# Third attention: tiles turned by ordinary matmuls with the identity as moving operand, and one step later

## What is computed

```python
Q, K, V = (proj(Wq), proj(Wk), proj(Wv))
scores = jnp.einsum('bhqd,bhkd->bhqk', Q, K) / SCALE
rel_k = pek[idx]
scores = scores + jnp.einsum('bhqd,qkd->bhqk', Q, rel_k) / SCALE
scores = jnp.where(causal[None, None], scores, -jnp.inf)
attn = jax.nn.softmax(scores, axis=-1)
out = jnp.einsum('bhqk,bhkd->bhqd', attn, V)
rel_v = pev[idx]
out = out + jnp.einsum('bhqk,qkd->bhqd', attn, rel_v)
```

## Time and profile before

| | us |
|---|---|
| median of 3 runs | 4647.89 |
| lowest and highest | 4644.03, 4655.52 |
| the profiled execution, its own time | 4653.93 |
| its span | 4652.1 |
| PE busy in the span | 3257.9 (70%) |
| DVE busy | 2404.9 (52%) |
| ACT busy | 1877.1 (40%) |

### The profile page before, as it was taken

How to read it: one execution, slowest core, us unless ns; L and a number is a source line. 1 busy time by engine, 2 the same in 40 slices (tenths; PEclk the granted TensorE clock), 3 DMA queues, 4 the chain that set the end, 5 groups by cost and what they waited for, 6 DMA issues and landing times. The chain is left out here.

```text
span 4652.1 us, 70787 instructions
## 1 busy us (share of the span) xinstructions
PE 3257.9 (70%) x22883; PEld 1799.3 (39%) x22883; DVE 2404.9 (52%) x4948; ACT 1877.1 (40%) x4450; POOL 684.5 (15%) x964
## 2 busy tenths in 40 slices
PE   5588544374435777778775777777783288849998
PEld 3344233253322444444443333333332122227776
DVE  4565466455655666666642445445455488821111
ACT  2355322211113455554542444444441177723332
POOL 2100000120003444444422000000000300000000
PEclk8798766686667899999986666666665599969999
DMA  4323000000001000000004777777772522220000
GB/s 118 64 48 62 23 0 0 8 1 5 0 9 47 17 17 9 17 17 17 17 9 138 188 190 192 190 192 191 193 195 72 137 42 53 40 69 1 0 0 18
DMA packets 423549, 303.19 MB, mean 65 GB/s; under 512 B 60175, under 2 KB 396234, under 8 KB 423250
## 3 DMA queue, kind: packets, MB, share of 16 engines
q1 hardware_dynamic: 414034, 278.32, 24.3%
q0 software_dynamic: 6912, 18.88, 1.3%
q10 hardware_dynamic: 2304, 2.36, 0.2%
HBM read 148.98 MB, written 133.18 MB: 61 GB/s over the span
## 5 line engine op out<-in xcount | busy, mean ns | idle before, releaser
L1139 DVE TENSOR_REDUCE a_soft_NM<-a_soft_s_ps 128x2 f32<-128x1024 f32 (+3 forms) x512 | 514.5, 1021 | 204.2 <-PE a_soft_s_ps L1074 132.3
L1173 ACT ACTIVATE a_soft_PTS<-a_soft_st_ps 128x512 f32<-128x512 f32 (+3 forms) x1024 | 458.3, 522 | 148.1 <-PE a_soft_st_ps L1050 100.9
L464 PE MATMUL a_soft_pt_ps<-net_ident,a_soft_PR 128*128 128x128 f32 x1280 | 328.7, 369 | 110.0 <-ACT a_soft_PTS L566 103.5
L612 ACT ACTIVATE a_soft_PR<-a_soft_s_ps,a_soft_least 128x128 f32<-128x128 f32 (+3 forms) x512 | 263.7, 526 | 342.3 <-DVE a_soft_least L587 237.9
L1045 PE MATMUL a_soft_st_ps<-a_soft_QS,a_soft_KS 50*128 50x512 bf16 (+4 forms) x1024 | 258.7, 360 | 59.4 <-ACT a_soft_PTS L1173 33.3
L1954 ACT ACTIVATE f_run_HT<-f_run_h_ps 128x512 f32<-128x512 f32 x256 | 152.8, 597 | 290.7 <-PE f_run_h_ps L1921 290.7
L1968 DVE SCALAR_TENSOR_TENSOR net_X<-f_run_y_ps,f_COEF,net_X 128x128 f32 x256 | 72.1, 344 | 381.2 <-PE f_run_y_ps L1930 381.2
L464 PEld LDWEIGHTS a_soft_pt_ps<-net_ident,a_soft_PR 128*128 128x128 f32 x1280 | 182.6, 180 | 208.7 <-ACT a_soft_PR L612 146.2
L1930 PEld LDWEIGHTS f_run_y_ps<-f_W,f_run_HT 128*128 128x128 f32 x2048 | 237.5, 192 | 26.8 <-issue 26.8
L1087 PE MATMUL a_soft_o_ps<-a_soft_PTS,a_soft_VR 128*32 128x512 f32 (+3 forms) x2048 | 242.6, 548 | 0.1
L2104 PE MATMUL f_run_ps<-f_run_WQKV,f_run_HT 128*128 128x512 f32 x384 | 229.6, 689 | 15.5 <-DVE f_run_RS L1402 8.3
(11 more groups left out here) (356 smaller groups left out, 6517.4 us busy)
## 6 DMA issues: line engine op xcount, KB each, us to landing
a_soft_BIAS<-skew_d SPq DMA_DIRECT2D x256, 191.0 KB, 4.2
band_d<-a_soft_PR SPq DMA_DIRECT2D x256, 191.0 KB, 3.7
skew_d<-a_soft_RS SPq DMA_DIRECT2D x128, 256.0 KB, 4.4
a_soft_PB<-band_d SPq DMA_DIRECT2D x128, 256.0 KB, 3.1
a_soft_QS<-query_rows_d SPq DMA_DIRECT2D x32, 384.0 KB, 9.6
query_rows_d<-a_proj_PARTS SPq DMA_DIRECT2D x72, 128.0 KB, 3.5
query_rows_d<-a_proj_PARTS POOLq DMA_DIRECT2D x72, 128.0 KB, 3.0
key_rows_d<-a_proj_PARTS SPq DMA_DIRECT2D x72, 128.0 KB, 3.9
```

Source lines behind the costliest of these rows:

```text
L464: last = pe.transpose(pt_ps[:, slot, kb * P:(kb + 1) * P], PR[:, n % NPR, OFF + kb * P:OFF + (kb + 1) * P], ident[:])
L612: act.activation(PR[:, n % NPR, OFF:OFF + width(j)], s_ps[:, n % 4, 0:width(j)], ACT.Exp, bias=least[:, n:n + 1], scale=-1.0).then_inc(pro ...
L1139: dve.tensor_reduce(NM[:, T % 2, j, p, :], s_ps[:, ring["s", a] % 2, :, 0:width(j)], AX.X, ALU.max, negate=True).then_inc(max_ready, 1)
L1173: act.activation(PTS[:, T % 2, 2 * p + par, kb, q0:S], st_ps[:, e % 3, q0:S], ACT.Exp, scale=scale).then_inc(probs_ready, 1)
```

## The change

Two things are changed in `relative_heads`:

1. `turn` and `turn_band` call `pe.matmul(out, lhsT=tile, rhs=ident, start=True, stop=True)` in place of `pe.transpose(out, tile, ident)`. The result is the same turned tile.
2. The turn in step n is that of step n-3 (LAG = 3). With it the tiles per position change: step j = 0 turns two tiles (one of them was three), j = 1 three, j = 2 four beside the band's four, j = 3 one. The semaphore counts in `missing`, `before`, `through`, `pv` and in ACT's wait before it writes `PR` follow, and so do the last turns after the last quad.

```diff
+    LAG = 3
     def missing(seq, slots):
-        return sum(m < seq and m % 2 in slots for m in (0, 1, 2, 7))
+        return sum(m < seq and m % 2 in slots for m in (0, 1, 2, 3, 7))
     def before(hd, pos):
-        return 5 * hd + pos - 4
+        return 5 * hd + pos - 5
     def through(qd, h, pos):
-        return 10 * qd + (5 * h + pos) // 2 - 2
+        return 10 * qd + (5 * h + pos) // 2 - 2 - (5 * h + pos) % 2
@@ turn
-                    last = pe.transpose(pt_ps[:, slot, kb * P:(kb + 1) * P], PR[:, n % NPR, OFF + kb * P:OFF + (kb + 1) * P], ident[:])
+                    last = pe.matmul(pt_ps[:, slot, kb * P:(kb + 1) * P], PR[:, n % NPR, OFF + kb * P:OFF + (kb + 1) * P], ident[:],
+                                     start=True, stop=True)
@@ turn_band
-                    last = pe.transpose(pt_ps[:, slot, j * P:(j + 1) * P], PB[:, hb % 2, j, :], ident[:])
+                    last = pe.matmul(pt_ps[:, slot, j * P:(j + 1) * P], PB[:, hb % 2, j, :], ident[:], start=True, stop=True)
@@ pv
-            def pv(qd, sl, kb, turned=2):
+            def pv(qd, sl, kb, turned=(2, 1)):
-                    pe.wait_ge(pt_copied[0], 10 * (qd + 1) + turned)
-                    pe.wait_ge(pt_copied[1], 10 * (qd + 1) + turned)
+                    pe.wait_ge(pt_copied[0], 10 * (qd + 1) + turned[0])
+                    pe.wait_ge(pt_copied[1], 10 * (qd + 1) + turned[1])
@@ quad of PE
-                    if n >= 2:
-                        turn(qd, n - 2, h, pos, qd)
+                    if n >= LAG:
+                        turn(qd, n - LAG, h, pos, qd)
                     elif prev:
-                        turn(qd - 1, n + 14, h, pos, qd)
+                        turn(qd - 1, n + 16 - LAG, h, pos, qd)
@@ last of PE
-                turn(4 * B - 1, 14, 0, 0, 4 * B)
-                turn(4 * B - 1, 15, 0, 1, 4 * B)
+                turn(4 * B - 1, 13, 0, 0, 4 * B)
+                turn(4 * B - 1, 14, 0, 1, 4 * B)
                 turn_band(4 * B - 1, 2, 0, 4 * B)
-                turn_band(4 * B - 1, 3, 0, 4 * B, 3)
+                turn(4 * B - 1, 15, 0, 3, 4 * B)
+                turn_band(4 * B - 1, 3, 0, 4 * B, 4)
@@ copies (n - 2 and n + 14 become n - LAG and n + 16 - LAG), last of DVE
+                copy_out(dve, 0, 4 * B, 0, 4, 1, 3, None)
@@ quad of ACT
-                        act.wait_ge(pt_ready, before(4 * qd + h - 2, 4 + j))
+                        act.wait_ge(pt_ready, before(4 * qd + h - 2, (5, 6, 7, 9)[j]))
```

More of the change, by code:

```diff
@@ L527, in last @@
             def last():
-                turn(4 * B - 1, 14, 0, 0, 4 * B)
-                turn(4 * B - 1, 15, 0, 1, 4 * B)
+                turn(4 * B - 1, 13, 0, 0, 4 * B)
+                turn(4 * B - 1, 14, 0, 1, 4 * B)
                 turn_band(4 * B - 1, 2, 0, 4 * B)
-                turn_band(4 * B - 1, 3, 0, 4 * B, 3)
+                turn(4 * B - 1, 15, 0, 3, 4 * B)
+                turn_band(4 * B - 1, 3, 0, 4 * B, 4)
                 for kb in range(NPT):
-                    pv(4 * B - 1, 1, kb, 0)
+                    pv(4 * B - 1, 1, kb, (1, -1))
             for hd in range(3):
@@ L548, in copies @@
                         copy_out(eng, slot, qd, h, pos, sl if h >= 2 else 1 - sl, (h + 2) % 4, None)
-                elif n >= 2:
-                    copy_out(eng, slot, qd, h, pos, sl, (n - 2) // 4, n - 2)
+                elif n >= LAG:
+                    copy_out(eng, slot, qd, h, pos, sl, (n - LAG) // 4, n - LAG)
                 elif prev:
-                    copy_out(eng, slot, qd, h, pos, 1 - sl, 3, n + 14)
+                    copy_out(eng, slot, qd, h, pos, 1 - sl, 3, n + 16 - LAG)
         def copy_out(eng, slot, now, h, pos, sl, head, n):
@@ L591, in last @@
             def last():
-                copy_out(dve, 0, 4 * B, 0, 0, 1, 3, 14)
+                copy_out(dve, 0, 4 * B, 0, 0, 1, 3, 13)
                 copy_out(dve, 0, 4 * B, 0, 2, 1, 2, None)
+                copy_out(dve, 0, 4 * B, 0, 4, 1, 3, None)
             batches(quad, last, dve)
@@ L640, in last @@
             def last():
-                copy_out(act, 1, 4 * B, 0, 1, 1, 3, 15)
-                copy_out(act, 1, 4 * B, 0, 3, 1, 3, None)
+                copy_out(act, 1, 4 * B, 0, 1, 1, 3, 14)
+                copy_out(act, 1, 4 * B, 0, 3, 1, 3, 15)
                 store(4 * B - 1, 1, B, 0)
```

## The result

The changed kernel takes 4779.2 us (median of four runs, 4772.3 to 4787.8) against 4646.0 for the kernel before, measured beside it: 1.028 times, 95% interval 1.026 to 1.030, or 130 us more. The forecast was 4631, the range 4615 to 4700. Sign and size were both wrong.

A forecast was written before the change was run, and what follows sets the result against it. SP's queue, waiting for band-store landings, was taken as the bound. Of its 25.1 us waiting for exponentials about 20 go, against 3 us added: net -17 us, 4631 on the median, range 4615 to 4700.

The forecast's parts named there:

- That SP bounds the kernel before: Third attention: SP's queue, waiting 354.8 us of 951 for band-store landings, sets the round; at most 29 us can be won.
- 0.1 us a quad, 3 us in all: Cost in the sum for the early step and the longer step with the band, against about 20 us won.
- Two records a tile: Turned tiles: an ordinary f32 matmul makes two PE records, not one; +0.11 us a tile at upper clock, +0.2 at lower.
- their 6 to 11 us of PE a quad: PE's extra time for 56 turned tiles a quad: +6.2 us all at the upper level, +11 all at the lower.
- LAG 3: I take 0: Turning tiles one step later: worth 0 to 0.3 us a quad, taken as 0, since ACT's slot copies still hold PE.
- at step 2 ... 0.5 to 1.4 us later, mostly under the wait for the key rows: Score matmul behind step 2's four-tile turn comes 0.5 to 1.4 us later, mostly hidden by PE's key-row wait.
- The clock: PE's granted clock over the third attention rises from 0.67 to near 0.9 or more, except around the two waits.
- nothing is lost in the low stretch: Steps 4 to 11: two 0.11 us records replace one of 0.21, other matmuls get faster; about -1 us on 15.1.
- PE becomes the bound: Rival, chance 0.17: low-clock heads take PE 8.4 us against SP's 7.0; two per quad give +90 us, 4738 (4665 to 4830).

The follow-up runs named there:

- the runs with the fill: Changed kernel plus eight 512-column matmuls per quad, result unread, in PE's step-2 wait: 4760.1 us (1.0236); also with output stores on POOL: 4756.7 us (1.0231).

## Why the prediction was wrong

*That SP bounds the kernel before* was right: moving its wait off gives 43 us, and making ACT quicker gives none. What failed is the use of it. The prediction measured slack as SP's small wait for exponentials and priced the compute side only against that: its sum has 0.1 us a quad, 3 us in all, for everything that the edit adds to the chain. The chain's own length without SP's wait was 28.5 us against 29.9 with it, so 1.4 us of slack, about 44 us in all, stood against an edit that lengthens the chain by 5.6 us a quad (28.5 to 34.1), 179 us in all. The rest, 135, is about the 130 measured. The prediction also took one quad's round, 28.9 us, as SP's own; the mean quad is 29.9.

*Two records a tile* was right, 2560 and 1024 of them on the page, as was their pitch: eight records in 1.06 us at the upper level, 2.05 at the lower. What failed is that their 6 to 11 us of PE a quad, which the prediction had worked out, went into the sum as nothing. Doubling the records alone, in transpose mode, costs 47 us at lag 2 (a single run) and 100 at lag 3.

*The step "LAG 3: I take 0"* failed. Its copies are as late as before, as said, but the lag also puts the four-tile turn on the band's step. In transpose mode that costs 45 us where no wait covers it. The prediction had the burst's size (1.8 us) and let it delay only the last exponential of a head, against SP's slack there. In fact it delays the work of DVE and ACT at every such step (by their order its copies come ahead of their next items): steps 2, 6, 10 and 14 grew by 6.5 us together, part of it the ordinary form.

*The step "at step 2 ... 0.5 to 1.4 us later, mostly under the wait for the key rows"* failed. The turn at step 2 took 1.6 us longer (2.05 for 0.45), and step 2 as a whole 2.35 us more. The key rows' wait did vanish, and gave back 1.8 us at step 4; that exchange was right in kind. What it overlooked is ACT: four issues took 2.47 us where they took 1.79, with an `issue` gap of 2.91, and they stand ahead of the copy that frees the slot. That place was worth 57 us.

*The clock* rose, as forecast, in part: 0.82 over the stage where I wanted 0.9 or more. The term that hung on it, about -1 us on the stretch from step 4 to the third head's last exponential ("nothing is lost in the low stretch"), failed. Steps 4 to 11 took 16.6 us before and 16.9 after, although the 1.8 us of step 4 came back: in the mean steps 3 to 6 still run low, and a turned tile costs two records there. The reason given was wrong too. The prediction read rows 1 (7.71 of 8.40 us busy with transposes, 0.50) as agreeing with the Trainium skill, "TensorE: Matmul & The Clock Gate", Part 4: PE-mode transpose, that transpose mode doesn't count as busy. Turned twice in transpose mode the stage reaches 0.83, so in this kernel it does count, and the measurement decides. The low level in rows 1 came after the waits at steps 2 and 4. A level bought with more records is paid for with those records. The advice of "Perfetto Trace Analysis", Transposes, in the Trainium skill, to turn by transposes and not by ordinary matmuls, holds here: ordinary matmuls cost 90 us at lag 2 once SP's wait no longer hides a part.

*The rival "PE becomes the bound"*, 4738 from two low heads a quad, had the sign and came nearest; it got 0.17. Its mechanism is not what the runs show: PE is busy 86% of the stage, and moving ACT's issues gives 57 us with PE's work unchanged. Its condition was met narrowly, though: 0.82 in the mean is 36% of the time at the lower level, about 1.4 heads of a quad, most of it in steps 3 to 6. It had priced two heads, so its nearness is in part luck. The bound is the order of PE, DVE and ACT, each waiting for the one before, and not PE's load alone.

What stays open: the 50 us that lag and ordinary matmuls cost only together. The low stretch of the clock, ACT's pause and the burst all play in, and the runs with the fill show that their prices don't add. How much of the loss is the low stretch itself is open too: the filled quads at full level last 28.5 to 29.8 us, which would make it large.

## What to carry to other kernels

When one queue is the floor, ask how long the other chain would be alone: its small wait for that chain shows that the chain is on time, not by how much. The cheap test is to take the queue's wait away (here by moving it to an idle queue), which shows both the slack and a gain. A stage that hands work around three in-order engines can pay for a burst in all three orders (here 45 us in transpose mode, with no tile more): don't put the largest turn on the step that already holds another. A higher clock is no gain when it comes from more work. And look at several rounds before reading one: here every fourth quad differs from its neighbours, and a row from it misleads.

## What the runs showed of the hardware

Transposes in transpose mode raised the granted clock like ordinary matmuls, once there were enough of them: 0.67 to 0.83 over the stage. An ordinary f32 tile's weight loads take 192 ns each against 142 for the transpose form (medians above), matmul records 275 against 273 ns.

At the start of every fourth quad, where the program's loop goes round, ACT stood longer. The kernel after:

```profile
2824.51 2.52 ACTq L631 DMA_DIRECT2D heads_d<-a_soft_OS  x4
2831.69 0.37 ACT L616 ACTIVATE a_soft_PR<-a_soft_s_ps,a_soft_least 128x128 f32<-128x128 f32 x1 [7.34 <-issue]
```

From the end of the issues to the exponential are 4.7 us, against 0.26 in the quad shown above, and step 2 of such quads takes over 10 us against 6. In the kernel before the same pause lay mostly under the wait for the key rows: step 2 of such quads takes 7.1 us against 3.8, but step 4 takes 1.5 against 4.0, and the quad 30.6 against 29.8. In the kernel after they take 37.6 us in the mean against 33.6, so about 16 of the 130 us are in these five quads alone. In the kernel with ordinary matmuls at lag 2 they are 6.0 us longer than in the kernel before and the others 0.7: 30 of its 48 us by the profiles. Without SP's wait such quads take 30.3 to 32.6 us in the kernel before, where the others of the loop take 27.2 to 29.0.

With the output issues on POOL the pause is still there, only smaller. From the last exponential of a quad to the first of the next it is 7.4 to 8.2 us at the loop's turn and 3.5 elsewhere in the kernel after; with the stores on POOL, 3.5 to 4.0 and 0.5. So it comes with the loop's turn: 4 us with ACT's issues ahead of it, 3 without. What ACT's queue does in it no run here shows.
